# A four-layer graph kernel: byte masks, node-major basis products, count products divided at written columns

## What is computed

```python
x = layernorm(x + rel(x))      # layer 1: per edge, 16 basis products, an attention weight, sum by dst
x = layernorm(x + A @ x)       # layer 2: plain sum over the edges
x = layernorm(x + gat(x))      # layer 3: softmax of leaky(s_src[src] + s_dst[dst]) over the edges of dst
x = layernorm(x + prop(x))     # layer 4: 10 steps f = 0.9 * D^-1/2 A S^-1/2 f + 0.1 * x
```

## Time and profile before

| | us |
|---|---|
| runs | 1407.72, 1410.02, 1411.17; median 1410.02 |
| profiled execution, its own time | 1406.4 |
| its span | 1404.6 |
| sweep, from the first line's use to the flags | 76 to 1018 |
| transposes, layer norm, layer 2 | 1021 to 1073 |
| scores and masks of layer 3 | 1074 to 1178 |
| final sums, layer norm, ten steps, end | 1180 to 1405 |

### The profile page before, as it was taken

How to read it: one execution, slowest core, us unless ns; L and a number is a source line. 1 busy time by engine, 2 the same in 40 slices (tenths; PEclk the granted TensorE clock), 3 DMA queues, 4 the chain that set the end, 5 groups by cost and what they waited for, 6 DMA issues and landing times.

```text
span 1404.6 us, 43341 instructions
## 1 busy us (share of the span) xinstructions
PE 1145.8 (82%) x16938; PEld 818.6 (58%) x16938; DVE 951.3 (68%) x3140; ACT 661.6 (47%) x1910; POOL 753.6 (54%) x793
## 2 busy tenths in 40 slices
PE   3279999999977888788878878878766895999995
PEld 2235555555544554455445545555455795999995
DVE  7277777777776667666766666667444999555555
ACT  1146666666655556555555555556501992000000
POOL 5777777777777777777777777777300000000000
PEclk9556677777666666766666667666758898999998
DMA  4521111112111111111111111110000000000000
GB/s 102 80 54 45 41 39 38 38 37 53 44 38 37 37 38 37 37 37 37 38 37 37 37 38 36 40 37 14 9 1 2 3 4 2 4 4 4 4 4 16
DMA packets 51171, 43.63 MB, mean 31 GB/s; under 512 B 34562, under 2 KB 47202, under 8 KB 50962
## 3 DMA queue, kind: packets, MB, share of 16 engines
q1 hardware_dynamic: 25938, 27.95, 6.9%
q0 software_dynamic: 25024, 12.86, 6.4%
HBM read 38.18 MB, written 2.57 MB: 29 GB/s over the span
## 4 chain that ended last, share of the span: by engine, by line
PE 34%; POOL 31%; DVE 17%; issue 12%; DMA 3%; SPq 1%; ACT 1%; ACTq 0%; DVEq 0%
POOL arena L485 31%; PE ps L681 15%; PE ps L638 7%; DVE arena L1242 6%; PE ps L597 2%; PE ps L621 2%; DVE arena L1088 2%; PE ps L605 2%; DVE arena L1086 1%; PE ps L592 1%; DMA arena<-x_pad,arena 1%; SPq L406 1%; DMA arena<-line_table 1%; DMA dst_parts<-arena 1%; DVE arena L1101 1%
## 5 line engine op out<-in xcount | busy, mean ns | idle before, releaser
L485 POOL DMA_INDIRECT arena<-x_pad,arena x782 | 751.8, 961 | 238.6 <-issue 236.4
L638 PE MATMUL ps<-arena,mix 128*32 128x80 f32 x1666 | 243.6, 320 | 0.6 <-ACT arena L845 0.6
L1088 DVE TENSOR_SCALAR arena<-pair_no,arena 128x275 bf16<-128x275 f16 (+2 forms) x784 | 239.4, 309 | 0.0
L605 PE MATMUL ps<-arena 128*128 128x275 bf16 (+1 forms) x784 | 156.9, 336 | 100.6 <-DVE arena L1088 100.1
L681 PE MATMUL ps<-arena,adj_words 128*128 128x64 f16 (+1 forms) x6875 | 215.8, 193 | 28.0 <-DVEq L1280 16.2
L681 PEld LDWEIGHTS ps<-arena,adj_words 128*128 128x128 fp8e4 x6875 | 213.2, 98 | 30.9 <-DVEq L1280 17.3
L638 PEld LDWEIGHTS ps<-arena,mix 128*32 128x32 f32 x1666 | 224.3, 147 | 4.5 <-ACT arena L845 1.0
L1101 DVE TENSOR_TENSOR arena<-ps,arena 128x132 f32<-128x132 f32 x196 | 57.1, 291 | 248.2 <-DMA arena<-x_pad,arena 133.1
L597 PE MATMUL ps<-arena 1*128 1x500 bf16 (+1 forms) x392 | 172.2, 440 | 30.5 <-DVEq L1064 20.7
L1116 DVE TENSOR_TENSOR arena<-ps,arena 128x768 f32<-128x768 f32 x196 | 187.9, 959 | 6.7
L621 PE MATMUL ps<-arena 128*32 128x187 f32 x1568 | 137.9, 435 | 21.2 <-DVE arena L1116 18.8
(11 more groups left out here) (187 smaller groups left out, 1243.5 us busy)
## 6 DMA issues: line engine op xcount, KB each, us to landing
arena<-line_table SPq DMA_DIRECT2D x28, 602.0 KB
arena<-x_pad,arena POOLq DMA_INDIRECT x782, 2.6
arena<-line_table SPq DMA_DIRECT2D x28, 140.0 KB
arena<-dst_parts SPq DMA_DIRECT2D x196, 5.7 KB
dst_parts<-arena SPq DMA_DIRECT2D x1, 918.8 KB, 11.5
feat_table<-rows SPq DMA_DIRECT2D x1, 800.0 KB, 13.8
x<-x_pad SPq DMA_DIRECT2D x1, 400.0 KB
out<-x SPq DMA_DIRECT2D x1, 400.0 KB, 4.9
```

The lines of the kernel that those rows point to most:

```text
L485: pool.indirect_dma_start(to, None, table, bass.IndirectOffsetOnAxis(ap=index, axis=0)).then_inc(done, 16)
L605: mm = nc.tensor.matmul(ps[:, at + first:at + first + n], row_hot[:, h, k, :], pair_hot[:, h, k, 0:n], start=False, stop=(k == SLOTS - 1))
L638: mm = nc.tensor.matmul(ps[0:FEAT, MOVED:MOVED + BATCH * PAGE], mix[:, m, :], sumsT[:, c % 2, :, m], start=(m == 0), stop=(m == MIXES - 1))
L1088: last = v.tensor_scalar(pair_hot[:, h, k, 0:n], pair_no[:, 0:n], pair_of[:, g, k:k + 1], None, ALU.is_equal)
```

## The change

What it does, part by part:

1. **Count products.** No clearing products. The first product into a bank (the carry, or slot 0 of group 0) has `start=True`, and each slot's product is divided at the column up to which the bank is already written, so that one part adds and the other writes fresh columns. Four products become eight for g >= 1.
2. **Mixed sums.** No clearing; each product has `start=True` and overwrites its own columns in its own 32 rows. Two zero products before the first group write the banks once.
3. **Basis products.** Operands exchanged: the sums are stationary (80 columns), basis m moving (32 columns); the result is [80 nodes, 32 features].
4. **Way of the sums.** ACT copies that result to one of six row pages (`copy_moved`, now after the page's group counts), SP stores each group's 20 rows in DRAM (`store_rows`, each waits for the one before to land, 24 groups behind its loads), and at the sweep's end loads the whole as `agg`. `to_nodes`, `to_agg` and the moves to `aggT` go; page moves run 2 groups late instead of 6.
5. **Masks.** `above` becomes a bitwise AND of mask bytes with the counts as 32-bit words (782 words). For 17 blocks DVE makes the bytes (255 or 0), for 8 (2, 5, ..., 23) ACT makes signs (-1, 0, 1), of which DVE drops the lowest bit; counts are limited to 8 for that, so the limit on the sum of squares goes from 256 to 64.
6. **Joined products.** For each pair (b, j) one product of `adj` with both fp16 parts of the small factors (66 columns, own banks 0 to 3) takes the place of two of 33 columns. The total of the small factors is subtracted from at the end instead of by negated copies.
7. **Degrees.** ACT sums the rows of `adj` for 5, 10 and 1 blocks before the first, before the second and after the second square root, and the rest between its masks.
8. **Final sums.** Per bank a product, a reduction over the two parts and a subtraction, then one product and one addition over all.

The core of the diff:

```diff
-DELAY = BATCH + 2
+DELAY = 2
+ROW_PAGES = 6
+STORE_DELAY = SIDES + 10
-ADJ_MAX = 16
+ADJ_MAX = 8
+BY_SCALAR = range(2, BLOCKS, 3)
+ALL_BUT_LOWEST = -16843010
+DEGREES_BEFORE = (5, 15, 16)
...
+                def store_rows(g):
+                    c, n = g // BATCH, g % BATCH
+                    base = sp.value_load(base_t[0:1, g:g + 1], min_val=0, max_val=NODES_PAD - PAGE)
+                    sp.wait_ge(moved_copied, c + 1)
+                    if g >= 1:
+                        sp.wait_ge(rows_paged, 16 * g)
+                    sp.dma_start(agg_table[bass.ds(base, PAGE), :], agg_rows[n * PAGE:(n + 1) * PAGE, c % ROW_PAGES, :])\
+                      .then_inc(rows_paged, 16)
...
+                    if g >= STORE_DELAY:
+                        store_rows(g - STORE_DELAY)
+                for g in range(GROUPS - STORE_DELAY, GROUPS):
+                    store_rows(g)
+                sp.wait_ge(rows_paged, 16 * GROUPS)
+                sp.dma_start(agg[:, 0:BLOCKS - 1, 0:FEAT], agg_table[0:(BLOCKS - 1) * P, :].rearrange("(b p) f -> p b f", p=P))\
+                  .then_inc(agg_loaded, 16)
...
+                    counted_to = 1 if g else 0
                     for k in range(SLOTS):
-                        first, n = STARTS[k] * BLOCKS, min(PAIR_DSTS[k], WIDTH) * BLOCKS
-                        mm = nc.tensor.matmul(ps[:, at + first:at + first + n], row_hot[:, h, k, :], pair_hot[:, h, k, 0:n],
-                                              start=False, stop=(k == SLOTS - 1))
+                        first, end = STARTS[k], STARTS[k] + min(PAIR_DSTS[k], WIDTH)
+                        for d0, d1 in ((first, counted_to), (counted_to, end)):
+                            if d1 > d0:
+                                mm = nc.tensor.matmul(ps[:, at + d0 * BLOCKS:at + d1 * BLOCKS], row_hot[:, h, k, :],
+                                                      pair_hot[:, h, k, (d0 - first) * BLOCKS:(d1 - first) * BLOCKS],
+                                                      start=(g == 0 and k == 0), stop=(k == SLOTS - 1 and d1 == end))
+                        counted_to = end
...
-                        clear(to, PAIRS)
...
-                        mm = nc.tensor.matmul(ps[0:FEAT, MOVED:MOVED + BATCH * PAGE], mix[:, m, :], sumsT[:, c % 2, :, m],
+                        mm = nc.tensor.matmul(ps[0:BATCH * PAGE, MOVED:MOVED + FEAT], sumsT[:, c % 2, :, m], mix[:, m, :],
                                               start=(m == 0), stop=(m == MIXES - 1))
...
-                pe.wait_ge(soft_parts_ready, 2)
+                pe.wait_ge(soft_parts_ready, 1)
                 for b in range(BLOCKS):
                     for j in range(BLOCKS):
-                        for h in range(2):
-                            nc.tensor.matmul(ps[0:rows_of(j), soft_at(j) + SOFT:soft_at(j) + 2 * SOFT],
-                                             adj[:, b, j * P:j * P + rows_of(j)], minus_small[:, b, h, :],
-                                             start=False, stop=False)
+                        nc.tensor.matmul(ps[0:rows_of(j), all_at(j):all_at(j) + 2 * SOFT], adj[:, b, j * P:j * P + rows_of(j)],
+                                         soft_parts[:, b, :, 1, :], start=False, stop=False)
...
-                    a.copy(agg_pages[:, c % 2, :], ps[0:FEAT, MOVED:MOVED + BATCH * PAGE]).then_inc(moved_copied, 1)
+                    if c >= ROW_PAGES:
+                        act.wait_ge(rows_paged, 16 * BATCH * (c - ROW_PAGES + 1))
+                    a.copy(agg_rows[:, c % ROW_PAGES, :], ps[0:BATCH * PAGE, MOVED:MOVED + FEAT]).then_inc(moved_copied, 1)
...
+                for n, b in enumerate(BY_SCALAR):
+                    if n >= 2:
+                        act.wait_ge(above_ready, BY_SCALAR[n - 2] + 1)
+                    a.activation(mask_signs[:, 2 + n % 2, 0:NODES], score_row[:, 0:NODES], ACT.Sign, bias=least[:, b:b + 1],
+                                 scale=-1.0).then_inc(scalar_masks, 1)
+                    if n >= 1:
+                        out_degrees(done, done + 1)
+                        done += 1
...
+                dve.wait_ge(agg_loaded, 32)
...
-                    v.scalar_tensor_tensor(out=above[:, b % MASKS, 0:NODES], in0=score_row[:, 0:NODES],
-                                           scalar=least[:, b:b + 1], in1=adj[:, b, 0:NODES],
-                                           op0=ALU.is_ge, op1=ALU.mult, saturate=False).then_inc(above_ready, 1)
+                    if b in BY_SCALAR:
+                        n = BY_SCALAR.index(b)
+                        dve.wait_ge(scalar_masks, n + 1)
+                        v.scalar_tensor_tensor(out=above_words[:, b % MASKS, 0:words], in0=mask_words[:, 2 + n % 2, 0:words],
+                                               scalar=all_but_lowest, in1=adj_ints[:, b, 0:words],
+                                               op0=ALU.bitwise_and, op1=ALU.bitwise_and).then_inc(above_ready, 1)
+                    else:
+                        n = own_done
+                        if n >= 1:
+                            dve.wait_ge(above_ready, own_blocks[n - 1] + 1)
+                        make_mask(n + 1)
+                        dve.wait_ge(masks_made, n + 1)
+                        v.tensor_tensor(above_words[:, b % MASKS, 0:words], mask_words[:, n % 2, 0:words],
+                                        adj_ints[:, b, 0:words], ALU.bitwise_and).then_inc(above_ready, 1)
+                        own_done += 1
```

More of the change, by code:

```diff
@@ L594, in fetch @@
                     mm.then_inc(fetched, 1)
-                def clear(at, cols):
-                    nc.tensor.matmul(ps[:, at:at + cols], nothing[:, 0:P], nothing[:, 0:cols], start=True, stop=False)
                 def count(g):
@@ L637, in times_bases @@
                     for m in range(MIXES):
-                        mm = nc.tensor.matmul(ps[0:FEAT, MOVED:MOVED + BATCH * PAGE], mix[:, m, :], sumsT[:, c % 2, :, m],
+                        mm = nc.tensor.matmul(ps[0:BATCH * PAGE, MOVED:MOVED + FEAT], sumsT[:, c % 2, :, m], mix[:, m, :],
                                               start=(m == 0), stop=(m == MIXES - 1))
                     mm.then_inc(moved_out, 1)
-                clear(COUNTS, PAIRS)
-                clear(MIXED, PAGE * MIXES)
+                for bank in range(2):
+                    nc.tensor.matmul(ps[:, MIXED + bank * BANK:MIXED + bank * BANK + PAGE * MIXES], nothing[:, 0:P],
+                                     nothing[:, 0:PAGE * MIXES], start=True, stop=True)
                 fetch(0)
@@ L714, in run_dense @@
                     mm.then_inc(above_used, 1)
-                for at in range(0, BLOCKS, SOFT_PER_BANK):
-                    mm = nc.tensor.matmul(ps[:, soft_at(at):soft_at(at) + SOFT_PER_BANK * 2 * SOFT], zero_row[0:1, 0:P],
-                                          zero_row[0:1, :], start=False, stop=True)
+                for at in SOFT_BANKS:
+                    mm = nc.tensor.matmul(ps[:, at:at + SOFT_PER_BANK * 2 * SOFT], zero_row[0:1, 0:P], zero_row[0:1, :],
+                                          start=False, stop=True)
                 mm.then_inc(soft_summed, 1)
@@ L891, in root, with out_degrees @@
                      .then_inc(d_root_out, 1)
+                def out_degrees(first, last):
+                    for b in range(first, last):
+                        a.activation(counted, adj[:, b, 0:NODES], ACT.Copy, accum_out=src_count[:, b:b + 1])\
+                         .then_inc(degree_out, 1)
+                        act.wait_ge(degree_out, b + 1)
+                first, second, third = DEGREES_BEFORE
+                out_degrees(0, first)
                 root(1)
+                out_degrees(first, second)
                 root(2)
+                out_degrees(second, third)
                 for c, (at, w) in enumerate(CHUNKS):
@@ L1238, in run_dense, with make_mask @@
                 dve.wait_ge(score_row_copied, len(CHUNKS))
+                own_blocks = [b for b in range(BLOCKS) if b not in BY_SCALAR]
+                words = -(-NODES // 4)
+                def make_mask(n):
+                    if n < len(own_blocks):
+                        b = own_blocks[n]
+                        v.tensor_scalar(mask_bytes[:, n % 2, 0:NODES], score_row[:, 0:NODES], least[:, b:b + 1], 255.0,
+                                        ALU.is_ge, ALU.mult).then_inc(masks_made, 1)
+                make_mask(0)
+                own_done = 0
                 for b in range(BLOCKS):
```

104 lines of the change are left out of this document (46 added, 58 removed).

## The result

The changed kernel takes 1394.49 us (median of 4 runs, 1394.01 to 1394.9) against 1410.60 us before on the same chip (4 runs, 1407.72 to 1413.02): ratio 0.9886, 95% interval 0.9867 to 0.9906. That is 16.1 us faster; 1393.5 was predicted. The profiled execution took 1394.01 us (span 1392.1) where that of before took 1406.4 (1404.6), 12.5 us in the span. So the two traces explain 12.5 us. The other 3.6 are there because the profiled execution of before lay 4.2 us under the median of these four runs and that of the changed kernel only 0.5.

What follows compares the result with a forecast made beforehand. Four stages in turn bound the kernel, with POOL's gathers bounding the sweep. Terms -0.8, -5.5, -14.4 and +4.2 make -16.5 us: 1406.4 profiled becomes 1389.9, or 1393.5 against the median; range 1383 to 1407.

Steps and rivals of the forecast that it cites:

- The bound of the sweep: Sweep: POOL's gathers set its end, so PE's saving of about 0.8 us per group counts as zero.
- the clears: Behind the last gather's landing: two clearing products fewer, less the split of count products, -0.8 us, bounds 0 and -1.8.
- the basis products: L638, end of the sweep: exchanging the operands changes nothing, bounds -0.4 and +2.5 us.
- L485 still ends near 1001 us: Sign to look for: the gathers end at the same time, whatever PE's share in the sweep.
- The sums by way of DRAM: Last basis product to first use of the sums: 14.1 us instead of 19.6, -5.5 us, bounds -9 and +6.
- So they hide by some 1 us, table load of 1.3 included.: Before the first square root: ACT's five degree sums, 1016 to 1031 us, end before the root is due at about 1033.5.
- rival C: SP's queue in the sweep: stores over 3.6 us each hold up line loads and gathers, 1443 us, chance 0.09.
- The mask stage: Masks to final sums: the bound moves from DVE to PE, 2.66 us a block, final sums start sooner, -14.4 us.
- Rivals B and D: Mask stage: byte masks at the slow rate, 1406 us, chance 0.13; joined products costing as two, 1407 us, chance 0.05.
- The final sums: After the last masked product: twelve operations plus two, 7.7 us against 3.5, all on the path, +4.2 us.
- The profiled execution against the median: Whole kernel: the profiled execution lay 3.6 us below the median, so 1389.9 became 1393.5 us.

Runs made afterwards that it cites:

- doubled stores: Changed kernel with each of its 196 stores of a group's sums issued twice: 1573.45 us, ratio 1.1166 to the kernel before.
- clears back: Changed kernel with both clearing products put back in every group, ahead of the carried product: 1396.42 us, ratio 0.9906 to the kernel before.
- joined products ahead: Changed kernel with square-root table loaded early, joined products three blocks ahead, their banks reduced early, shorter final sums: 1387.55 us, ratio 0.9839 to the kernel before.
- sweep alone: Kernel before with only the sweep's part of the change, masks as before; run twice on slower chips: 1692.11 and 1695.39 us, ratios 0.9855 and 0.9858.
- masks alone: Kernel before with only byte masks, joined products, early degree sums and new final sums; twice on slower chips: 1712.18 and 1713.71 us, ratios 0.9963 and 0.9958.

## Why the prediction was right, point by point

The time was met (1394.5 for 1393.5), and each part went by the mechanism that was forecast, but for one step (point 3), with terms that were off both ways. That it was met to a microsecond is luck (point 7).

1. *The bound of the sweep, the clears, the basis products.* Right. PE's busy time fell by 0.5 us a group and not 0.8 (from 163 to 143 us in 200, or 39.5 groups), at a lower clock; it is hidden all the same. The last basis product takes 4.99 us instead of 4.97. What lies behind the last gather gave 0.6 us of the 0.8. "L485 still ends near 1001 us": the last gather started at 1003.5; in another execution of the same sweep it did at 1001.4.
2. *The sums by way of DRAM*, -7.7 for -5.5. The mis-sized terms are the store and the reload: the four stores took 1.4, 1.4, 1.7 and 1.8 us from start to start (2.1 taken), the reload 3.93 (5.0). The Trainium skill, *DMA: Bandwidth & Descriptors*, Anatomy of one DMA, has some 2.0 us fixed for a DMA on GpSimd's path, mostly the write receipt. The stores here are issued by SP, which that section does not speak of. This trace has 1.2 us from issue to landing for three of the four last stores of 2.5 KB into DRAM, so for them the measurement decides for less.
3. *"So they hide by some 1 us, table load of 1.3 included."* This step failed. The five degree sums did end in time (1032.77, 2.1 us ahead of the root's data), but the load was counted as if it would go in front of the wait, where it stands in the kernel before. Behind the degree sums it stands behind the wait. It costs 1.3 us, and one more instruction gives them back.
4. *SP and rival C.* The outcome was right and the margin was not. The round was put at 27.7 us of 34.8 with a limit of 3.6 us a store. Its waits for PE show 4.2 us to spare in a mean round, and doubled stores 4.1, where the prediction saw 7.1. (The 34.8 us was one round; the mean is 33.8.) The sum of the round took the store once behind the line load and then 2.2 us a group; the pitch is 2.66, because load and store each take SP 1.33.
5. *The mask stage*, -11.9 for -14.4. The mechanism held in each of its steps: byte mask 1.84 us (1.85), AND 0.97 (0.97), first masked product 4.5 us after the start (4.8), PE without a gap to 1161.6, DVE waiting 8.6 us for it, norm factors hidden. The size failed in two terms. From 1096.3 to 1161.6 us PE did 1200 masked and 575 joined products; the masked at 35.4 ns leave 39.7 for a joined one, 0.99 us a block for 0.885, and over 23 blocks that is 2.5 us. The 75 products ahead of them took 4.4 us, 0.6 more than at the 50 ns taken, 0.2 of which comes back because 90 had been put at that rate. The start and the closings gave 0.2 each. Rivals B and D are out by these rows.
6. *The final sums*, +3.8 for +4.2: twelve operations of 0.29 to 0.63 us and two of 1.02.
7. *The profiled execution against the median.* Before's lay 3.6 us below its median and 3.6 were added. Medians moved by 16.1 us and spans by 12.5, which is again 3.6. The forecast owes its closeness to this and to errors that cancel: the sum -16.5 against the profile's own -12.5 is 4 us off, 3.4 of which is the start of the last gather. The other errors (+0.2, -2.2, +1.3, -1.2, +2.5, -0.4, +0.3) nearly cancel. It may be that before's profiled execution lay below its median just because its gathers were short (961 ns, in the other traces of the usual chips 962 to 967); one trace can't show it.

## What to carry to other kernels

When work is put ahead of an activation that waits, look where its table load went. Here it ran ahead of the wait as long as the root was ScalarE's first work in the dense part, and behind the wait once degree sums stood ahead of it. An activation of one column of the same function, issued while the engine is idle, moved it out of the path. When the bound goes from one engine to the next, look at once at both ends of the new one: here the wait ahead of the first product and the sums behind the last were worth another 6 us. Sum up a serial queue's round by the pitch of its issues in the trace and not by its landings, over many rounds, and read its room from what it waits for; doubling the suspected load checks that.

## What the runs showed that was not expected

**More work, lower clock.** In the same 200 us of the sweep the kernel before has 163 us of PE and a granted clock of 0.67, the changed one 143 us and 0.54, and the one with clears back 200 us and 0.50, the lower level throughout. Busy time does not tell the clock here (part of it is itself the lower clock), and neither of the two moved the end of the sweep by more than the 1.5 us of the clears.

At the start of the mask stage the clock is 0.50 from 1087.3 to 1094.9 us, then 0.70, and 1.00 from 1096.3 on:

```profile
1091.90:1094.90 3.00, 2.99 (x50) 2.83 (x50) 3.00 (x3) 1.78 (x2) 0.00 (x0) 0.50 0.03 5
1094.90:1096.30 1.40, 1.40 (x29) 1.30 (x28) 1.40 (x2) 0.64 (x1) 0.00 (x0) 0.70 0.00 0
1096.30:1098.00 1.70, 1.70 (x51) 1.62 (x50) 1.70 (x2) 1.70 (x1) 0.00 (x0) 1.00 0.00 0
```

In joined products ahead, where PE has no wait there, it is at 0.50 up to 1092.0 and at 1.00 from there on. That is 5.2 us behind the stage's first product, where the changed kernel takes 9.0. So part of what filling the wait gives is the clock.

**Chips on which every kernel takes 300 us longer.** Waits in 600 to 800 us of the sweep (us in total, times, longest), first the changed kernel on the usual chip, then the sweep's part alone on the third lot's:

```profile
ACT arena L891 <- DVE arena L1137: 61.8, 30, 6.0
DVE arena L1136 <- DMA arena<-x_pad,arena: 49.9, 23, 5.4
```
```profile
DVE arena L1108 <- remote: 80.5, 16, 8.7
ACT arena L864 <- remote: 34.9, 8, 6.8
POOL arena L507 <- remote: 31.3, 24, 2.3
...
PEld ps L644 <- issue: 23.5, 31, 1.3
```

DVE, ScalarE and POOL stand for up to 8.7 us with a releaser that the records don't name, PE has gaps of up to 1.3 us that no releaser explains, and only 129 gathers fall into the 200 us (158 on the usual chip). A gather itself is hardly longer (963 to 975 ns in the eight traces, 961 to 967 on the usual chips), and the stages behind the sweep are as long as ever. What makes the sweep slow there was not tried. Nor is it shown why the sweep's part gives 22 to 23 us on these chips. What the traces do show is that the gathers don't set the sweep's end there: from the start of the last one to the last weight load of the basis products 88.6 us pass in sweep alone and 91.5 to 92.1 in masks alone, where it is 12.7 on the usual chip. So what the change takes out of PE's and ScalarE's queues can count.
